# Biases of q, k and v in empty rows of the convolution, and the projection in front of the scores

## What is computed

```python
def layer(x):                       # x = _gn(x) of the input; the result is added to the input
    xw = windows of 16x16 of x      # 64 windows for each of the 4 images
    q = shuffle_invert(conv3(xw, qw, qb), 2)    # 32 channels -> 128 features, 64 tokens
    k = shuffle_invert(conv3(xw, kw, kb), 2)
    v = shuffle_invert(conv3(xw, vw, vb), 2)
    q, k, v = ln(q) * SCALE, ln(k), ln(v)       # over the 128 features, with gains and biases
    attn = softmax(q @ k.T + bias)              # 8 heads of 16, 64 x 64
    out = (attn @ v) @ proj_w.T + proj_b
    xr = image of (xw + pixel_shuffle(out, 2))
    return xr + conv3(gelu(conv3(xr, c1w, c1b)), c2w, c2b)
```

## Time and profile before

| what | value |
|---|---|
| median of 3 runs | 811.42 us |
| the profiled execution: its time | 810.2 us |
| the profiled execution: its span | 808.4 us |
| PE (TensorE matmul) busy | 744.3 us (92%), 5898 instructions |
| DVE (VectorE) busy | 657.2 us (81%) |
| ACT (ScalarE) busy | 569.1 us (70%) |
| POOL busy | 491.9 us (61%) |
| granted TensorE clock, mean | 0.993 |

### The profile page before, as it was taken

One profiled execution on the slowest core, in us unless ns is written; L12 is line 12 of the kernel. 1 busy time (PEld: TensorE's weight loads), 2 busy tenths in 40 slices (PEclk: granted clock), 3 DMA queues, 4 the chain that ended last, 5 costly groups with the idle time before them and its releaser, 6 DMA issues.

```text
span 808.4 us, 18167 instructions
## 1 busy us (share of the span) xinstructions
PE 744.3 (92%) x5898; PEld 549.4 (68%) x5898; DVE 657.2 (81%) x2150; ACT 569.1 (70%) x1191; POOL 491.9 (61%) x1041
## 2 busy tenths in 40 slices
PE   0469999999899999999899999999999999999988
PEld 0247877777556778877555778777655688787753
DVE  6549889897859899897967989899775989887675
ACT  1399888767367988876547978876737788878630
POOL 6368778741457788763346777874244778886210
PEclk9999999999999999999999999999999999999999
DMA  7112331000013161000101332100101314000002
GB/s 266 59 30 60 96 144 60 2 1 23 38 65 97 33 239 44 18 1 1 59 33 54 110 125 116 60 1 2 56 5 66 98 32 135 2 2 2 2 1 104
DMA packets 17662, 47.32 MB, mean 59 GB/s; under 512 B 2080, under 2 KB 2720, under 8 KB 17568
## 3 DMA queue, kind: packets, MB, share of 16 engines
q1 hardware_dynamic: 17568, 46.15, 16.7%
HBM read 37.76 MB, written 8.39 MB: 57 GB/s over the span
## 4 chain that ended last, share of the span: by engine, by line
PE 67%; DVE 12%; ACT 9%; issue 5%; POOL 5%; DMA 0%; SPq 0%; POOLq 0%; ACTq 0%; DVEq 0%
PE y_ps L1015 18%; PE o_bank L1081 9%; PE s_ps L1056 8%; PE pt_ps L1069 7%; PE y_ps L982 4%; PE s_ps L1097 3%; PE t_ps L1040 3%; PE ox_ps L1138 3%; PE o_bank L1138 3%; PE pt_ps L1138 3%; PE s_ps L1138 3%; PE y_ps L1010 2%; DVE h_lo L505 2%; DVE h_hi L502 2%; ACT qk_n L855 1%
## 5 line engine op out<-in xcount | busy, mean ns | idle before, releaser
L743 POOL TENSOR_TENSOR sc<-sc,mx 128x512 f32<-128x512 f32 x128 | 133.7, 1044 | 59.9 <-DVE mx L568 59.9
L855 ACT ACTIVATE qk_n<-y_ps,ln_nr,ln_rs 128x128 f32<-128x128 f32 x256 | 104.4, 464 | 88.4 <-POOL ln_nr L733 88.2
L1015 PE MATMUL y_ps<-w_hi,x_hi 128*128 128x192 f16 (+1 forms) x512 | 147.2, 287 | 0.0
L1015 PE MATMUL y_ps<-w_hi,x_lo 128*128 128x192 f16 (+1 forms) x512 | 146.9, 287 | 0.0
L1015 PE MATMUL y_ps<-w_lo,x_hi 128*128 128x192 f16 (+1 forms) x512 | 146.7, 287 | 0.0
L541 DVE BATCH_NORM_STATS2 ln_st<-y_ps 128x6 f32<-128x128 f32 x384 | 88.8, 287 | 60.1 <-PE y_ps L1015 58.9
L1081 PE MATMUL o_bank<-v_bd,pt 128*128 128x66 f32 x1024 | 129.1, 269 | 3.9 <-DVE on L589 3.8
L1081 PEld LDWEIGHTS o_bank<-v_bd,pt 128*128 128x128 f32 x1024 | 124.4, 192 | 5.5 <-DVE pt L575 4.7
L730 POOL TENSOR_TENSOR ln_rs<-ln_ve,neg_half 128x3 f32<-128x3 f32 x128 | 113.4, 886 | 10.7
L870 ACT ACTIVATE sc<-sc 128x512 f32<-128x512 f32 x128 | 82.8, 647 | 39.3 <-POOL sc L743 39.3
L863 ACT ACTIVATE v_bd<-y_ps,ln_vs 128x128 f32<-128x128 f32 x256 | 105.2, 475 | 0.0
(11 more groups left out here) (190 smaller groups left out, 1607.7 us busy)
## 6 DMA issues: line engine op xcount, KB each, us to landing
xs<-in_x_sh_dram SPq DMA_DIRECT2D x32, 576.0 KB, 4.4
xst<-in_x_al_dram SPq DMA_DIRECT2D x16, 512.0 KB, 8.2
xf<-in_x_al_dram SPq DMA_DIRECT2D x32, 256.0 KB, 5.2
out_dram<-xf SPq DMA_DIRECT2D x32, 256.0 KB, 2.0
wst<-in_wqkv_dram SPq DMA_DIRECT2D x1, 768.0 KB, 4.2
w1s<-in_w_dram SPq DMA_DIRECT2D x1, 256.0 KB, 8.7
w2s<-in_w_dram SPq DMA_DIRECT2D x1, 256.0 KB, 8.7
biasS<-in_bias_t_dram SPq DMA_DIRECT2D x1, 256.0 KB, 9.6
```

The costliest lines, as they stand in the source:

```text
L743: pool.tensor_tensor(sc[i % 4][:, :, :, :], sc[i % 4][:, :, :, :], mx[i % 2][:, :, :].unsqueeze(2).to_broadcast([P, HP, TOK, 2]), ALU.subt ...
L855: ins = act.activation(qk_n[j][:, t, :].rearrange("p (h y x) -> p h y x", h=HEADS, y=2), by_head(y_ps[j][:, E * t:E * (t + 1)]), ACT.Identity,
L1015: ins = pe.matmul(y.rearrange("p (t e) -> p t e", t=3)[:, :, cols], xx[r % 2][:, s, a % 2, 2 * TS * (a // 2):2 * TS * (a // 2 + TS)], ww[: ...
```

## The change

The bias moves into the empty rows. x_u holds, for each column phase, the 96 useful rows of x_hi that shift 1 reads, and in the other 32 rows constants; w_b holds shift 1's weights, with three parts of the bias in those rows. Two matmuls of 192 columns, one for each phase, take the place of the bias matmul and of the hi-hi product of shift 1; each writes every second column of y_ps. The constants in x_u are written once; the 96 rows are copied for each row of windows by two DMAs, 96 partitions with four runs of 128 fp16 each, which wait for x_hi. POOL prepares the parts and w_b at the start with 17 operations; VectorE takes one maximum and one more link in place of a cast. One load, of the ones, goes.

The projection on TensorE moves in front of the scores of its step; it waits for the addition of the position bias of the step before (`p0 + i` in place of `p0 + (i + 1)`). VectorE's addition to xr moves to directly behind the maximum. SP's order of loads and stores is rewritten around the copies. ScalarE's program is as it was.

```diff
@@ sync @@
+            def with_bias_rows(b, r):
+
+                sp.wait_ge(xhi_done, (b * NROW + r) * 2 + 2)
+                for x in range(2):
+                    rows = slice(32 * x, 32 * x + 96)
+                    sp.dma_start(x_u[r % 2][rows, x, :, :], x_hi[r % 2][rows, :, 1, 0:2 * TS * TS]).then_inc(
+                        loaded_u[r % 2], 16)
...
             def image(b, followed):
-                for r in range(4, NROW):
-                    row(b, r)
+                for r in range(3, 6):
+                    row(b, r + 2)
+                    with_bias_rows(b, r)
...
                     load_image(b + 1)
-                    for r in range(4):
+                with_bias_rows(b, 6)
+                with_bias_rows(b, 7)
+                if followed:
+                    for r in range(2):
                         row(b + 1, r)
-                for t in range(T2N):
-                    sp.wait_ge(y_ready, b * T2N + (t + 1) + 1)
-                    sp.dma_start(out[b, :, 512 * t:512 * (t + 1)], xf[t][:, :]).then_inc(stored, 16)
+                    for r in range(2):
+                        with_bias_rows(b + 1, r)
+                        row(b + 1, r + 2)
+                for t in range(5):
+                    store(b, t)
+                if followed:
+                    row(b + 1, 4)
+                    with_bias_rows(b + 1, 2)
+                for t in range(5, T2N):
+                    store(b, t)
@@ vector, step @@
                     v.tensor_reduce(mx[i % 2][:, :, :], sc[i % 4][:, :, :, :].rearrange("p h k w -> p h w k"), AX.X,
                                     ALU.max).then_inc(maxed, 1)
+                if i % 4 == 0 and i >= 8:
+                    r = (i - 8) // 4
+                    v.wait_ge(proj_done, r0 + (r + 1))
...
+                        v.tensor_tensor(rows, rows, s_ps[:, :, 256:512].rearrange("p w (n j) -> p w n j", j=TS),
+                                        ALU.add).then_inc(xr_added, 1)
...
                     ins.then_inc(normed, 1)
 
-                if i % 4 == 0 and i >= 8:
-                    r = (i - 8) // 4
-                    v.wait_ge(proj_done, r0 + (r + 1))
...
@@ gpsimd, start @@
-            for j in range(3):
-                bias_link(pool.tensor_copy(b_tmp[:, :], bst[:, :]))
-                bias_link(pool.tensor_copy(b_parts[32 * j:32 * j + 32, :], b_tmp[32 * j:32 * j + 32, :]))
-                bias_link(pool.tensor_tensor(bst[:, :], bst[:, :], b_tmp[:, :], ALU.subtract))
+            bias_link(pool.tensor_scalar(b_part[0][:, :], bst[:, :], 1.0 / B_STEPS[0], None, ALU.mult))
+            bias_link(pool.tensor_scalar(b_tmp[:, :], b_part[0][:, :], B_STEPS[0], None, ALU.mult))
+            bias_link(pool.tensor_tensor(bst[:, :], bst[:, :], b_tmp[:, :], ALU.subtract))
+            bias_link(pool.tensor_copy(b_part[1][:, :], bst[:, :]))
+            bias_link(pool.tensor_tensor(bst[:, :], bst[:, :], b_part[1][:, :], ALU.subtract))
+            bias_link(pool.tensor_scalar(b_part[2][:, :], bst[:, :], 1.0 / B_STEPS[2], None, ALU.mult))
+            pool.wait_ge(w_hi_done, 3)
+            by_phase = lambda t: t.rearrange("p (n x) -> p x n", x=2)
+            bias_link(pool.tensor_copy(w_b[:, :, :], by_phase(w_hi[:, 1, :])))
+            for j in (2, 1, 0):
+                for x in range(2):
+                    rows = slice(96 * (1 - x), 96 * (1 - x) + j + 1)
+                    bias_link(pool.tensor_copy(w_b[rows, x, :], by_phase(b_part[j][:, :])[rows, x, :]))
+            for t in x_u:
+                for x in range(2):
+                    rows = slice(96 * (1 - x), 96 * (1 - x) + 32)
+                    bias_link(pool.tensor_copy(t[rows, x, :, :].rearrange("p m t -> p (m t)"),
+                                               vec[rows, BROW:BROW + 1].to_broadcast([32, NPAIR * P])))
@@ tensor, step @@
-                    pe.matmul(y, ones_b[0:96, :], b_parts[0:96, :], start=True, stop=False)
-                    for a in range(4):
+                    for a in (2, 0, 3, 1):
...
-                        for xx, ww in ((x_hi, w_hi), (x_hi, w_lo), (x_lo, w_hi)):
+                        for xx, ww in ((x_hi, w_hi), (x_hi, w_lo), (x_lo, w_hi))[a == 1:]:
...
+                    if s == 0:
+                        pe.wait_ge(loaded_u[r % 2], 32 * (rr0 + r // 2 + 1))
+                    for x in range(2):
+                        ins = pe.matmul(y.rearrange("p (n x) -> p x n", x=2)[:, x, :],
+                                        x_u[r % 2][:, x, s, :], w_b[:, x, :],
+                                        start=False, stop=x == 1)
                     ins.then_inc(conv_done, 1)
...
                         ins = pe.transpose(t_ps[:, t, m % 2, :], qk_n[m % 2][:, t, :], idf[:, :])
                     ins.then_inc(tr_done, 1)
 
+                if i % 4 == 0 and i >= 8:
+                    r = (i - 8) // 4
+                    pe.wait_ge(ot_copied, r0 + (r + 1))
+                    if r < 6:
+                        pe.wait_ge(biased, p0 + i)
...
+                    ins.then_inc(proj_done, 1)
                 if has(i):
                     h = i // 2
                     pe.wait_ge(qkt_done, h0 + (h + 1))
...
-                if i % 4 == 0 and i >= 8:
-                    r = (i - 8) // 4
-                    pe.wait_ge(ot_copied, r0 + (r + 1))
-                    if r < 6:
-                        pe.wait_ge(biased, p0 + (i + 1))
...
```

More of the change, by code:

```diff
@@ L42 @@
 GN_BOUND = float(IMG)
-GQ, BQ, GK, BK, GV, BV, PB, C1B, EVEN, ODD, C2B, EVEN2, ODD2, WIN0, WIN1, GVP, GVP1, BVP, BVP1 = range(19)
-NVEC = 19
+GQ, BQ, GK, BK, GV, BV, PB, C1B, EVEN, ODD, C2B, EVEN2, ODD2, WIN0, WIN1, GVP, GVP1, BVP, BVP1, BROW = range(20)
+NVEC = 20
 T1R = 5
@@ L84, in conv_attention @@
         bst = sb("bst", [P, QKV])
-        b_parts = sb("b_parts", [P, QKV], BF16)
-        b_tmp = sb("b_tmp", [P, QKV], BF16)
+        b_part = [sb(f"b_part{j}", [P, QKV], F16) for j in range(3)]
+        b_tmp = sb("b_tmp", [P, QKV])
+        b_max = sb("b_max", [P, 3])
+        w_b = sb("w_b", [P, 2, QKV // 2], F16)
+        x_u = [sb(f"x_u{i}", [P, 2, NPAIR, P], F16) for i in range(2)]
         biasS = sb("biasS", [P, 2, HP * TOK])
@@ L171, in conv_attention @@
         bias_split = sem("bias_split")
+        b_maxed = sem("b_maxed")
+        loaded_u = [sem(f"loaded_u{i}") for i in range(2)]
         c_scaled = sem("c_scaled")
@@ L333, in _ @@
                 load(dst, src, loaded_consts)
-            for r in range(2, 4):
-                row(0, r)
+            for r in range(2):
+                with_bias_rows(0, r)
+                row(0, r + 2)
+            row(0, 4)
+            with_bias_rows(0, 2)
             images(image)
@@ L569, in step @@
                                     ALU.max).then_inc(maxed, 1)
+                if i % 4 == 0 and i >= 8:
+                    r = (i - 8) // 4
+                    v.wait_ge(proj_done, r0 + (r + 1))
+                    if i == 8:
+                        v.wait_ge(xr_begun, b * 4 + 5)
+                    rows = xr[:, TS * r:TS * (r + 1), :].rearrange("p i (m w j) -> p w (i m) j", w=2, j=TS)
+                    if r < 6:
+                        v.tensor_tensor(rows, rows, s_ps[:, :, 256:512].rearrange("p w (n j) -> p w n j", j=TS),
+                                        ALU.add).then_inc(xr_added, 1)
+                    else:
+                        for w in range(2):
+                            ins = v.tensor_tensor(rows[:, w, :, :], rows[:, w, :, :],
+                                                  proj_bank[r][w].rearrange("p (n j) -> p n j", j=TS), ALU.add)
+                        ins.then_inc(xr_added, 1)
                 if has(i - 2):
@@ L1009, in step @@
                     y = y_ps[m % 2][:, 0:QKV]
-                    pe.matmul(y, ones_b[0:96, :], b_parts[0:96, :], start=True, stop=False)
-                    for a in range(4):
+                    for a in (2, 0, 3, 1):
                         cols = {0: slice(0, E // 2), 3: slice(E // 2, E)}.get(a, slice(0, E))
-                        for xx, ww in ((x_hi, w_hi), (x_hi, w_lo), (x_lo, w_hi)):
[L1015 to L1018, removed]
+                        for xx, ww in ((x_hi, w_hi), (x_hi, w_lo), (x_lo, w_hi))[a == 1:]:
+                            pe.matmul(y.rearrange("p (t e) -> p t e", t=3)[:, :, cols],
+                                      xx[r % 2][:, s, a % 2, 2 * TS * (a // 2):2 * TS * (a // 2 + TS)],
+                                      ww[:, a, :].rearrange("p (t e) -> p t e", t=3)[:, :, cols],
+                                      start=(a == 2 and ww is w_hi and xx is x_hi), stop=False)
+                    if s == 0:
[4 more added lines that the diff above has]
+                                        start=False, stop=x == 1)
                     ins.then_inc(conv_done, 1)
@@ L1041, in step @@
                     ins.then_inc(tr_done, 1)
+                if i % 4 == 0 and i >= 8:
+                    r = (i - 8) // 4
```

(15 more changed lines are left out.)

56 lines of the change are left out of this document (18 added, 38 removed).

## The result

The changed kernel takes 870.4 us (median of four runs), the kernel before 811.4 in the same measurement: 1.0716 times as long, with a 95% interval of [1.0701, 1.0731]. One of the four runs, at 907.7 us with a granted clock of 0.85, was in a slower state and is left out of the ratio. Forecast were 851 us, from 828 to 866. The sign is right, and the result lies 4 us above the range. The profiled execution took 870.41 us, with a span of 868.6; the 59 us more are the subject here, 19 of them not forecast.

The account below looks back on a forecast made before the run. TensorE bounds, VectorE about a microsecond per four-step group behind. Lag 4 x 11.0, less convolution savings 3 x 1.6 and 0.2, plus start 0.9, gives +39.9 on the profiled 810.2; median offset 1.2 makes 851 us, range 828 to 866.

Parts of the forecast that it names:

- The late copy: Moved projection on TensorE waits for ScalarE's ot six times per image, 1.2 to 3 us each.
- VectorE's lag: Bias additions delayed behind the moved projection; 16.4 us less recovered waits leaves 11.0 us per image, four images.
- the 0.8 us that step 31 was to give back: Step 31's wait of 0.82 us for the scores, expected to be eaten, reducing each image's loss.
- VectorE's waits for the convolutions would nearly vanish: Sign of being right: VectorE waits for the scores, some 2 to 3 us in projection steps, instead of for convolutions.
- TensorE's busy time falls by some 20 us: Sign of being right: TensorE's total work shrinks by some 20 us although the span grows.
- So I charge nothing for the step.: New convolution matmuls writing every second fp32 of y_ps were priced like contiguous ones, 0.17 us for two.
- new matmuls further apart than 0.09 us: Sign of being wrong: spacing of the two 192-column convolution matmuls above 0.09 us.
- the saving: Convolution 0.16 us less per pair, counted outside the groups: 1.6 us in three images, 0.2 in the first.
- the double price: Rival: the step in y_ps doubles the new matmuls, 0.17 us more per pair, removing the gain; 856 us, chance 0.10.
- the start at +0.9: POOL's nine bias operations become 17 at the start, delaying the inverse behind them by 0.9 us.
- The copy is in time: Rival: ot is ready at the projection's turn and TensorE stays the bound; about 794 us, chance 0.12.
- TensorE stalls, VectorE keeps up: Rival: VectorE recovers, so only TensorE's stalls of 10.8 us per image count; 839 us, chance 0.14.

Follow-up runs that it names:

- e5: e2 plus ten unread matmuls of 248 columns in front of each TensorE wait for the copy ot: 855.4 us, 1.0551 times before.
- e2: Kernel before with only the projection moved in front of the scores and VectorE's addition to xr behind the maximum: 867.7 us, 1.0700 times before.
- e9: Changed kernel plus ten unread matmuls of 248 columns in front of each TensorE wait for the copy ot: 856.5 us, 1.0583 times before.
- e4: e1 with q, k and v columns reordered so each new matmul writes three runs of 64 fp32: 797.8 us, 0.9842 times before.
- e3: Changed kernel with q, k and v columns reordered so each new matmul writes three runs of 64 fp32: 870.0 us, 1.0727 times before.
- e1: Changed kernel with the projection and VectorE's addition to xr back at their old places, only the bias change left: 811.9 us, 1.0015 times before.
- e7: e2 with ScalarE's copy ot moved in front of the previous step's normalisation of q, k and v: median 817.7 us, ratio 1.0042.

## Why the prediction was right and wrong

**The late copy: right, and in size.** Forecast were waits of 1.23, 1.74 three times, 2.77 and 1.56 us; the rows of after show 1.20, 1.92, 1.91, 1.72, and for the last two 2.76 and 1.78. Groups were to take 19.2 us and take 19.0 at the full clock; what stands from the end of the copy to the bias addition is 1.67 us (88.53 to 90.20), put at 1.85. VectorE's lag was worked out as 44.0 us; e5, with the clock nearly restored, leaves 855.4 - 811.6 = 43.8. The parts hold too: in e5's first image the bias addition falls 1.7 us further behind in each of the three groups from step 8 to 20 (worked out as 1.9), 2.4 from step 20 to 24 (2.5) and 1.8 from 24 to 28 (1.6). Only the 0.8 us that step 31 was to give back did not come: from step 28 to 31 it is 13.2 us before, in e5 and in the kernel after. That VectorE's waits for the convolutions would nearly vanish holds in the body (0.9 us in the stretch above; in the same steps of the kernel before, 86 to 145, 4.0) and not elsewhere: over the span they fell only from 58.9 to 50.6.

**The step that failed most: TensorE's matmuls at the durations of before.** The sum took every matmul of TensorE's as long as before, so that a lower clock stood in it at nothing, without a reason. It noted that TensorE would idle six times per image, and never asked what TensorE does after idling. The runs put 12.3 us (e2 less e5) to 13.9 us (after less e9) on the lower clock behind those waits, some two thirds of the miss of 19. A rough estimate from the clock alone agrees: a mean of 0.976 over 868.6 us is 42 us at the lower level (0.024 x 868.6 x 2), before it was 11 (0.007 x 808.4 x 2); half of the 31 us more, 15 us, is what the same matmuls take longer, and that is lost wherever they are not waiting in any case. So "TensorE's busy time falls by some 20 us" failed twice, by slower matmuls and by the next point.

**The second step that failed: "So I charge nothing for the step."** The rows it rested on the earlier trace rows are fp32 matmuls, 297 ns with the step against 286 without; for fp16 the step takes 355 ns against 252, and 0.34 us for two against 0.17. That is the forecast's own sign of being wrong, new matmuls further apart than 0.09 us. I named the reason for doubt, that the fp32 columns pass more slowly there, and still went by the nearer shape and not the nearer type. The Trainium skill's page "PSUM — Partial Sum Buffer" (Specifications) says that non-contiguous patterns slow matmuls significantly; the measurement agrees for this step, and not for runs of 32 or 64, which cost nothing in e4. In the forecast the saving was worth 5.0 us, so with the double price the sum is 44.9, and with the 13.9 us of e9 58.8, where 59.0 were measured. That it comes out so closely is in part luck. That the saving is worth 5.0 us in this kernel is not shown: e3, with the short writes, is no faster by its median, and 4.4 us only between two single runs at the same clock.

**Right and small.** The copies into x_u at zero (2.3 us to landing, 5 us of cover); the start at +0.9, where the first normalised input is 0.7 us later (25.96 against 25.23) and e1 is 0.8 slower; the eight matmuls of the projection at 1.06, now 1.13. The 0.03 us for the semaphore stands in no row; from the end of the copy to the projection the kernel after shows 0.05 (88.53 to 88.58). Two slips change nothing: four times 4.04 and 1.06 make 17.22 and not 17.33, and the double price is 5.0 us with the first image, not 4.8.

**The rivals.** "The copy is in time" was refuted by the 24 waits; e7 shows that its case exists one edit away, in ScalarE's order. "TensorE stalls, VectorE keeps up" (+26.5) falls with e5: without the clock's share the loss is 43.8.

The range ended at 866 because its upper end was made of late starts and of the double write; a mechanism that was not in the list could not widen it.

## What to carry to other kernels

Before an instruction is moved ahead on an in-order engine, look when its operand's producer runs on its own engine, and move the producer first: putting a copy in front of the Exp and the normalisations of the step before was worth 50 us here, the move of its reader alone cost 57. When a forecast puts idle time into TensorE, add the slower matmuls behind it as a term of their own, bounded by rows of the same trace at both clock levels. Price a stepped PSUM write by a row of the same type, and where the layout of the features is free, choose it so that each matmul writes runs: with the projection left at its old place, that made the bias in the empty rows a gain of 1.6%.

## What I had not expected of the hardware

A step of two fp32 in PSUM doubles the time of a 192-column fp16 matmul (two in 0.34 us against 0.17) and hardly touches fp32 matmuls of 128 columns (297 ns, against 286 for transposes without the step). And TensorE, busy 18.1 of 20 us (119.5 to 139.5), still fell to the lower level behind a wait of 1.9 us, to a mean granted clock of 0.91, though not behind each such wait; ten useless matmuls in those waits, 1.2 us of work, gave back 12 to 14 us.
